# Pacing the edge-feature gathers of two attention layers by the softmax, and storing them from SyncE

## The reference, cut to what matters

```python
edge_index = jnp.stack([src, dst])
x = _layernorm(x + _L0_gnn_ref(x, ..., edge_index))                 # mean over neighbours
x = _layernorm(x + _L1_gnn_ref(x, edge_index, Wq, ...))             # two attention layers, 8 heads
x = _layernorm(x + _L2_gnn_ref(x, edge_index, edge_weight, W, b))   # normalised convolution
x = _layernorm(x + _L3_gnn_ref(x, edge_index, edge_attr_128, ...))  # messages with edge features
```

```python
# L1, for l in range(2): softmax over the edges of a target, for each of 8 heads
scores = jnp.einsum('ehd,ehd->eh', q[tgt], k[srcidx])
w = exp(scores - max over the target's edges) / (their sum + 1e-16)
agg = jax.ops.segment_sum(w[:, :, None] * v[srcidx], tgt, num_segments=n)
# L3: each edge has 128 features of its own, which are embedded and added to the source's row
edge_emb = edge_attr @ W_edge + b_edge
msg = jax.nn.relu(node_feats[src] + edge_emb)
aggr = jax.ops.segment_sum(msg, dst, num_segments=N)
```

## Time and profile before

| | |
|---|---|
| Median of three executions | 3275.06 us |
| Profiled execution: span | 3276.3 us |
| PE busy | 2543.2 us, 78% |
| DVE busy | 2052.8 us, 63% |
| ACT busy | 1712.5 us, 52% |
| POOL busy | 1057.7 us, 32% |
| Softmax blocks of the first layer, first to last start of the exponent | 979.5 to 1464.6 us |
| Softmax blocks of the second layer | 1657.1 to 2133.1 us |
| Gathers of features, first start to last | 977.5 to 1903.1 us |

### The profile page before, as it was taken

How to read it: one execution, slowest core, us unless ns; L and a number is a source line. 1 busy time by engine, 2 the same in 40 slices (tenths; PEclk the granted TensorE clock), 3 DMA queues, 4 the chain that set the end, 5 groups by cost and what they waited for, 6 DMA issues and landing times. The chain is left out here.

```text
span 3276.3 us, 44409 instructions
## 1 busy us (share of the span) xinstructions
PE 2543.2 (78%) x12731; PEld 1985.7 (61%) x12731; DVE 2052.8 (63%) x4101; ACT 1712.5 (52%) x3755; POOL 1057.7 (32%) x1063
## 2 busy tenths in 40 slices
PE   6125989998994349998952499987879999998778
PEld 4114855556883239995841389954756666666566
DVE  9104889999631118884521189847658887886666
ACT  2105898887621117771320177723158787873561
POOL 2771000003317770000067710011166666650111
PEclk9557999999996559999965599998989999999889
DMA  2000210002243432211333552111367776670201
GB/s 76 2 2 1 67 43 0 0 0 81 87 153 100 118 97 49 55 32 52 144 100 95 114 80 49 38 52 39 109 197 203 208 208 203 208 170 33 72 22 38
DMA packets 116593, 278.10 MB, mean 85 GB/s; under 512 B 24039, under 2 KB 38314, under 8 KB 116462
## 3 DMA queue, kind: packets, MB, share of 16 engines
q0 software_dynamic: 51328, 138.78, 15.8%
q1 hardware_dynamic: 65134, 137.65, 13.8%
HBM read 208.80 MB, written 59.43 MB: 82 GB/s over the span
## 5 line engine op out<-in xcount | busy, mean ns | idle before, releaser
L1404 ACT CAST pt_high<-bank 128x640 fp32r<-128x640 f32 x320 | 220.0, 688 | 432.1 <-remote 292.2
L1441 DVE TENSOR_TENSOR pt_low<-bank,pt_high 128x640 fp32r<-128x640 f32 x320 | 263.2, 823 | 283.1 <-ACT pt_high L1404 222.9
L2081 POOL DMA_INDIRECT x_got<-table_dram,src_idx x352 | 349.0, 992 | 210.8 <-DVE msg L2225 111.5
L1355 PE MATMUL bank<-ident,p 128*128 128x128 f32 x1600 | 254.4, 295 | 153.8 <-issue 79.1
L791 POOL DMA_INDIRECT feature_rows<-in_edge_attr,ids x352 | 335.9, 954 | 114.0 <-issue 108.0
L2225 DVE TENSOR_TENSOR msg<-bank,x_got 128x512 f32<-128x512 f32 x352 | 236.3, 682 | 125.7 <-PE bank L2106 97.4
L1355 PEld LDWEIGHTS bank<-ident,p 128*128 128x128 f32 x1600 | 204.3, 152 | 180.8 <-issue 117.9
L1435 DVE CUSTOM_DVE_ANT_0 p<-bank,log_counts 128x1254 f32<-128x1254 f32 x160 | 233.0, 1456 | 101.2 <-remote 71.5
L743 ACT ACTIVATE hot_rest<-hot_dst,slot_w 128x128 bf16<-128x128 bf16 x864 | 272.9, 399 | 38.4 <-DVE hot_dst L693 38.4
L572 PE MATMUL bank<-row_hot,col_part 125*128 125x352 f32 x840 | 166.6, 349 | 157.9 <-ACT col_part L615 97.7
L1337 PE MATMUL bank<-keys,queries 128*128 128x418 f32 x480 | 202.1, 421 | 104.3 <-DVE bound L1435 60.6
(11 more groups left out here) (436 smaller groups left out, 6419.5 us busy)
## 6 DMA issues: line engine op xcount, KB each, us to landing
features_dram<-feature_rows POOLq DMA_DIRECT2D x88, 256.0 KB
edge_got<-features_dram SPq DMA_DIRECT2D x88, 256.0 KB
qk_dram<-qk_high SPq DMA_DIRECT2D x16, 640.0 KB, 2.9
qk_dram<-qk_low SPq DMA_DIRECT2D x16, 640.0 KB, 4.2
keys<-qk_dram SPq DMA_DIRECT2D x32, 320.0 KB, 4.0
queries<-qk_dram SPq DMA_DIRECT2D x32, 320.0 KB, 5.8
queries_low<-qk_dram SPq DMA_DIRECT2D x32, 320.0 KB
acc_a<-zeros SPq DMA_DIRECT2D x1, 6400.0 KB, 30.5
```

What stands on the lines that cost most here:

```text
L1355: t = pe.transpose(unit(i)[:, j * P:(j + 1) * P], p[:, n % AHEAD, (u * HALF + j) * P:(u * HALF + j + 1) * P], k.ident[:])
L1404: act.copy(p_high[:, made % 3, :, n % 2 * P:(n % 2 + 1) * P], unit(2 * n + u).rearrange("p (j n) -> p j n", n=P)).then_inc(high_made, 1)
L1441: dve.tensor_tensor(p_low[:, made % 3, :, columns], unit(2 * n + u).rearrange("p (j n) -> p j n", n=P), p_high[:, made % 3, :, columns].bi ...
L2081: pool.indirect_dma_start(out=xg[:, g % XRING, j, :], out_offset=None, in_=k.table_dram, in_offset=bass.IndirectOffsetOnAxis(ap=k.src_idx[ ...
```

## The change

POOL issues the gathers alone. From the third pair of a layer on, each second gather of a group waits until the softmax has done the same share of its 80 blocks as POOL has done of its 176 gathers: gather t waits for `exp_done` at `t * 80 // 176`. The prefetch over two groups is gone; a group waits for the store of the group that had its place in the ring. The stores go to SP: in each head, ahead of that head's tile loads, SP waits for the groups that are due by then and stores them; the last ones come behind the load of the output weights, and SP waits for all stores at the layer's end in place of POOL.

```diff
-    def gather(self, pool, l):
-        k, ids, rows = self.k, self.ids, self.rows
-        first, ahead = l * LAYER_GROUPS, FRING // 2
-        end = first + LAYER_GROUPS
-        def load(g):
+    def gather(self, pool, l, exp_done):
+        ids, rows = self.ids, self.rows
+        first = l * LAYER_GROUPS
+        pool.tensor_copy(ids[:], k_ids(self.k, first)).then_inc(self.staged, 1)
+        gate(pool, self.staged, l + 1, self.passed)
+        for g in range(first, first + LAYER_GROUPS):
+            if g >= FRING:
+                gate(pool, self.saved[g % FRING], 16 * (g // FRING), self.passed)
             for j in range(GT):
                 t = (g - first) * GT + j
+                if j % PACED == 0 and pace(t):
+                    gate(pool, exp_done, pace(t), self.passed)
                 pool.indirect_dma_start(out=rows[:, g % FRING, j * ED:(j + 1) * ED], ...).then_inc(self.got[g % FRING], 16)
-        pool.tensor_copy(ids[:], k.id_idx[:, first * GT:end * GT]).then_inc(self.staged, 1)
-        gate(pool, self.staged, l + 1, self.passed)
-        for g in range(first, first + ahead):
-            load(g)
-        for g in range(first, end):
-            if g + ahead < end:
-                if g + ahead >= first + FRING:
-                    gate(pool, self.saved[(g + ahead) % FRING], 16 * ((g + ahead) // FRING), self.passed)
-                load(g + ahead)
-            gate(pool, self.got[g % FRING], 16 * GT * (g // FRING + 1), self.passed)
-            pool.dma_start(k.features_dram[g, :, :], rows[:, g % FRING, :]).then_inc(self.saved[g % FRING], 16)
+    def keep(self, sp, l, i):
+        g = l * LAYER_GROUPS + i
+        sp.wait_ge(self.got[g % FRING], 16 * GT * (g // FRING + 1))
+        sp.dma_start(self.k.features_dram[g, :, :], self.rows[:, g % FRING, :]).then_inc(self.saved[g % FRING], 16)
+    def all_saved(self, sp, l):
         for u in range(FRING):
-            gate(pool, self.saved[u], 16 * end // FRING, self.passed)
+            sp.wait_ge(self.saved[u], 16 * (l + 1) * LAYER_GROUPS // FRING)
+PACED = 2
+def pace(t):
+    return t * BLOCKS // (LAYER_GROUPS * GT)
...
         def _(pool):
-            features.gather(pool, l)
+            features.gather(pool, l, exp_done)
         @block.sync
         def _(sp):
-            for h in range(1, H):
-                if h >= 2:
+            at.load_tiles(sp, 1)
+            kept = 0
+            for h in range(2, H + 1):
+                while kept < LAYER_GROUPS and pace((kept + 1) * GT - 1) < (h - 1) * NB - 2:
+                    features.keep(sp, l, kept)
+                    kept += 1
+                if h < H:
                     sp.wait_ge(scored, place["scores", (h - 1) * NB - 1] + 1)
-                at.load_tiles(sp, h)
+                    at.load_tiles(sp, h)
             sp.wait_ge(half_done, 2 * HALF * (H - 1))
             at.load_wo(sp, 0)
+            for i in range(kept, LAYER_GROUPS):
+                features.keep(sp, l, i)
+            features.all_saved(sp, l)
```

More of the change, by code:

```diff
@@ L805, in gather, with k_ids @@
-        for u in range(FRING):
-            gate(pool, self.saved[u], 16 * end // FRING, self.passed)
+    def keep(self, sp, l, i):
[3 more added lines that the diff above has]
+    def all_saved(self, sp, l):
+        for u in range(FRING):
+            sp.wait_ge(self.saved[u], 16 * (l + 1) * LAYER_GROUPS // FRING)
+def k_ids(k, first):
+    return k.id_idx[:, first * GT:(first + LAYER_GROUPS) * GT]
```

## The result

The changed kernel takes 2973.16 us (median of four executions, 2968.1 to 2977.25), the kernel before on the same chip 3272.1 us (four, 3258.6 to 3282.57). The ratio is 0.9083, with a 95% interval of 0.9056 to 0.911: 299 us less. I had said 2929 (2880 to 3070). The profiled execution took 2976.51 us, its span 2974.8.

What follows compares the result with a forecast made beforehand. It took PE's semaphore signals, late while POOL issues gathers without a pause, to bound attention: 3276.3 - 389.5 (stall) + 38 (runs of eight) + 5 (start) = 2930 us, 2929 for the median; 80% range 2880 to 3070.

Steps and rivals of the forecast that it cites:

- The stall and its cause: Both attention layers: POOL's unbroken gathers make PE's semaphore signals late; pacing removes up to 389.5 us.
- only the rate counts: Rival, attention: the stall is a toll per gather, however spaced, so 106 us come back; 2998 us, chance 19%.
- What comes back: Attention: doubled pairs give a run of eight gathers once in ten blocks, 8 per layer, costing 38 us.
- The 5 us for the start: First blocks of a layer, before the ring is in step, a little slower than 3.43 us; 5 us for both layers.
- Six are free: Read from the message stage: a run of about six gathers without a pause costs nothing.
- run of eight costs 2.4 us: Read from the message stage: eight gathers without a pause cost 2.4 us, the price used for attention.
- The ring at the layer's end: Behind block 68 SP holds the stores; POOL may stop a few us and catches up; price 0.
- Stores to SP, and the end: Attention: stores ahead of SP's tile loads delay nothing, and the layer's end has cover of 4 to 8 us; price 0.
- No effect: Rival: the slow attention stretch has another cause, such as a layer's start or its loads; 3276 us, chance 3%.

Runs made afterwards that it cites:

- E4: The changed kernel without gathers in attention: SP copies contiguous rows into the same ring and stores them as before; 2893.14 us.
- E5: The changed kernel without the gathers' wait for the softmax, the stores still on SP; 3251.9 us.
- E2: The changed kernel with only the first of each eight gathers waiting for the softmax, at the same average pace; 3114.15 us.
- E1: The changed kernel with every gather, not each second one, waiting for its share of the softmax blocks; 2976.52 us.
- E3: The changed kernel with the stores back on POOL, one group behind its gathers, and the pace kept; 2923.94 us.
- E9: The changed kernel with its last stores ahead of SP's wait for the last halves, on the second chip; 2638.4 us, ratio 1.0007 to the kernel before.
- E6: The changed kernel with the wait for the softmax replaced by one for the last but one gather's landing, at most two in flight; 3028.89 us.
- E8: The changed kernel with the pace rounded otherwise, so the blocks that release four gathers come five blocks away from before; 2978.69 us.

## Why the prediction was right, and where not

**The stall and its cause.** Right, on a chip that behaves like that of the profile before. I had 389.5 us of stall. Against the floor of E4 the kernel before has 485.1 + 476.1 - 286.8 - 287.8 = 386.6 us. The time alone did not decide for it: 2973 us lies 44 us above the forecast and 25 under the rival "only the rate counts" (2998). The experiments do. E5 shows that the pace takes the stall away and E2 that the average rate does not: a run's length decides. The late starts behind PE's matmuls are in the timeline again, at the fourth or fifth gather of each run. That it is the signal that comes late, and not the matmul that ends late, is a reading: a matmul's end is modelled, and no run parts the two.

**What comes back.** The mis-sized term is the 38 us for the runs of gathers; measured are 325.4 + 325.0 - 286.8 - 287.8 = 75.8 us over the floor of E4, twice as much, and 325 us a layer where the forecast had it within 300. (The 5 us for the start are part of that floor and about right: in E4 the first four blocks take 15.8 and 15.6 us in the two layers, where four quiet ones take 13.7.) The runs are mostly of six gathers, with a short pause and a pair behind them, and not of eight as forecast. Two readings of the message stage failed in the term. "Six are free": E1's runs of five already cost some 2 to 2.8 us each (40 and 38 us over the floor in its layers, with 28 runs of five or more and 12 of four in both together). And the "run of eight costs 2.4 us" was DVE's idle time before one instruction of another stage; in the tight ring of the attention it is 5.1 us (E2). A count that fits several kernels, called an estimate, is 1.25 us, one gather, for each gather beyond the fourth: 5.0 us for eight (E2: 5.1), 10, 20, 25 and 35 for 12, 20, 24 and 32 (E5: 10.7, 17.6 to 19.1, 26.6 to 27.3, and 31.9), and 2.5 to 5 for the six to eight in the changed kernel (about 4). For the 176 of the kernel before, which has no pause, it gives 215 us in the first layer; measured are 198.3. For E1's five it gives 1.25 us, about half of what is measured, so it is rough. Read so, PE's ring stands from the fourth gather until the run ends.

**The ring at the layer's end.** Priced at nothing, "catches up". It does, but by eight gathers in a row: the block of 8.3 us and its neighbours are some 7 us per layer, a part of the 75.8. E3, without this stop, has no such block there (5.8 us at most). The edit that takes it away alone (E9) ran only where there is no hold.

**Stores to SP, and the end.** Price 0 held: no tile load is late in the changed kernel, and the first layer still ends with DVE's division (1320.14 to 1321.6). E6 shows what lies behind that cover: once POOL falls behind the softmax, late tiles stop PE for up to 9.4 us. What I did not see is what the stores did on POOL. Waiting there for the landing of the group before cut the runs (E3), and moving the stores costs 49 us against keeping them beside the pace.

**Elsewhere.** Outside the two layers the changed kernel has 2324.4 us, before 2315.1. These 9.3 us I had not; E4, E8 and E1 (2316.5, 2316.9, 2318.4) do not have them, E3 (2325.4) does. They are about as much as executions of the changed kernel differ by (2968.1 to 2977.25), and stay open. The sum closes: 3276.3 - 386.6 + 75.8 + 9.3 = 2974.8 us, the span.

**"No effect"** got 3%, and another chip brings it about: 1.0007 in E9. Nothing in the profile before could tell that its stall belonged to the chip, so that the forecast met a chip with the stall was luck. Between the chips the changed kernel (with E9's edit) differs by 339 us of span: 177 up to the first exponent, 74 in the two layers, and 88 in the rest, mostly the message stage. The kernel before differs by 635.

**The skill's rule.** It says that a DMA never contends with a compute engine ("SBUF — State Buffer", "Who interferes with whom", in the Trainium skill). The second chip agrees, with 287.7 us for the first layer with the gathers. On the first chip the rule gives the wrong time, 485.1 us for that layer in the kernel before. Its words are on ports, and the instructions themselves are no slower there: ACT's copy L1404 takes 692 ns beside the gathers and 686 without, DVE's L1435 1465 and 1454 ns. It is their starts that are late. The bytes are not what matters: the scatter stage moves 2 to 3 GB/s on both chips.

## What to carry to other kernels

When an engine that has its inputs starts late, with "remote" as releaser, and only while POOL issues indirect DMAs, look at how many it issues without a pause; pairs with 0.7 us or more behind them cost nothing here, five and more in a row did. Pace them by the consumer's progress, look where its shares double up, and look what the waits that you take off POOL did for it: one of them cut its runs; but do not wait for each landing, which made POOL too slow. And take such a stall to a second chip before you tune for it: this change is worth 9% on one, and with E9's edit nothing on the other.

## What the runs showed of the hardware

The two chips issue alike: a gather of the first layer takes 944 ns on the first (median of 176, the changed kernel) and 943 on the second (E9), one of the scatter stage's 152 indirect DMAs 978 ns on both. What differs is how soon DVE and ACT start behind PE's work meanwhile. In the scatter stage DVE's placing of the records idled 152.6 us in three waits on "remote" in the changed kernel on the first chip; on the second no such wait is listed:

```profile
L429 DVE TENSOR_SCALAR col_part<-row,slot_row,rec x252: 330/342/622, 66.0 to 448.9; 125x128 fp32r<-125x128 f16 x126
...
  remote: 152.6, 3
  PE bank L572: 34.5, 11
```

```profile
L429 DVE TENSOR_SCALAR col_part<-row,slot_row,rec x252: 327/339/619, 65.7 to 268.5; 125x128 fp32r<-125x128 f16 x126
...
  PE bank L572: 10.4, 9
```

The message stage's 352 additions take 570.5 us on the first (2084.5 to 2655.0) and 488.9 on the second (1827.6 to 2316.5), at 205 and 238 GB/s. Why the chips differ, whether it is the chip or a state that it was in, and whether E3, the best on the first chip, loses anything on the second, no run shows.
